# The last product of the scan moves from GpSimd to VectorE, and an output projection moves behind the last sums on TensorE

## The reference, cut to what matters

```
def step(h, inps):
    dt_t, x_t, B_t, C_t = inps
    dA = jnp.exp(dt_t[..., None] * A)
    h = h * dA + (dt_t * x_t)[..., None] * B_t[:, None, :]
    y = jnp.einsum('bdn,bn->bd', h, C_t)
    return (h, y)
_, ys = jax.lax.scan(step, h0, xs)
y = jnp.moveaxis(ys, 0, 1)
y = y + xc * D_param
y = y * jax.nn.silu(z)
mamba_out = y @ out_proj_w.T
residual = mamba_out + residual
hs = rmsnorm(residual, ln_ff_w)
...                                   # router, top 2 of 8 experts, experts
```

## Time and profile before

| | |
|---|---|
| median of three executions | 639.96 us (639.33 to 641.60) |
| profiled execution, device time | 641.04 us |
| its span, first to last instruction | 639.3 us |
| mean granted TensorE clock | 0.991 |
| PE busy | 592.2 us, 93% |
| DVE busy | 460.7 us, 72% |
| ACT busy | 387.9 us, 61% |
| POOL busy | 293.8 us, 46% |
| scan (first to last product on POOL) | 80.1 to 231.8 us |

### The profile page before, as it was taken

How to read it: one execution, slowest core, us unless ns; L and a number is a source line. 1 busy time by engine, 2 the same in 40 slices (tenths; PEclk the granted TensorE clock), 3 DMA queues, 4 the chain that set the end, 5 groups by cost and what they waited for, 6 DMA issues and landing times.

```text
span 639.3 us, 11082 instructions
## 1 busy us (share of the span) xinstructions
PE 592.2 (93%) x3725; PEld 466.4 (73%) x3725; DVE 460.7 (72%) x770; ACT 387.9 (61%) x876; POOL 293.8 (46%) x232
## 2 busy tenths in 40 slices
PE   4999779988999999999999999999999999999774
PEld 2653679988898888798889889899855555655442
DVE  6989989999999956534435442642575698999985
ACT  4589899999999956532223231311546665768543
POOL 6023599999999992222231333152113233133301
PEclk9999799999999999999999999999999999999998
DMA  8001552212121108424413441411520000000001
GB/s 283 2 1 36 159 222 63 55 52 65 50 59 58 34 7 331 138 111 173 162 52 149 158 172 41 165 34 33 172 108 1 2 1 0 1 2 1 1 0 66
DMA packets 18193, 51.44 MB, mean 80 GB/s; under 512 B 3779, under 2 KB 9540, under 8 KB 16485
## 3 DMA queue, kind: packets, MB, share of 16 engines
q1 hardware_dynamic: 15172, 41.43, 18.7%
q0 software_dynamic: 2688, 7.34, 4.0%
q10 hardware_dynamic: 288, 2.10, 0.9%
HBM read 45.95 MB, written 4.92 MB: 80 GB/s over the span
## 4 chain that ended last, share of the span: by engine, by line
PE 67%; ACT 13%; DVE 9%; issue 5%; DMA 3%; POOL 1%; POOLq 0%; DVEq 0%; ACTq 0%
PE ps L2067 13%; PE ps L2140 8%; PE ps L2075 7%; ACT arena L653 7%; PE ps L2129 4%; PE ps L2161 3%; ACT arena L668 3%; DMA moe_out<-arena,result_now 3%; PE ps L1884 3%; PE ps L1869 3%; PE ps L1966 2%; PE ps L1915 2%; PE ps L1710 2%; PE ps L2090 2%; PE ps L1719 2%
## 5 line engine op out<-in xcount | busy, mean ns | idle before, releaser
L442 POOL TENSOR_TENSOR arena<-arena 128x1024 f32<-128x1024 f32 x64 | 149.5, 2381 | 4.1 <-DVE arena L1262 3.8
L1262 DVE TENSOR_TENSOR_SCAN arena<-arena,ps 128x1024 f32<-128x1024 f32 x64 | 143.5, 2278 | 4.7 <-ACT arena L653 1.4
L2067 PEld LDWEIGHTS ps<-arena 128*128 128x128 f32 x924 | 106.1, 192 | 5.2 <-issue 4.1
L2067 PE MATMUL ps<-arena 128*128 128x128 f32 x924 | 107.4, 276 | 0.9 <-DVE arena L1360 0.3
L839 ACT ACTIVATE arena<-ps 128x256 f32<-128x256 f32 x63 | 24.1, 383 | 107.3 <-PE ps L2067 107.3
L653 ACT ACTIVATE arena<-arena,a_neg 128x510 f32<-128x510 f32 x128 | 84.6, 710 | 1.9 <-DVE arena L1262 1.7
L1869 PE MATMUL ps<-ident,arena 128*128 128x128 f32 x384 | 65.0, 279 | 9.9 <-ACT arena L664 9.0
L1884 PE MATMUL ps<-ident,arena 128*128 128x128 f32 x512 | 67.0, 273 | 2.2 <-DVE arena L1271 1.8
L668 ACT ACTIVATE arena<-arena,b_tok 128x512 f32<-128x512 f32 x96 | 64.9, 710 | 0.0
L1884 PEld LDWEIGHTS ps<-ident,arena 128*128 128x128 f32 x512 | 57.9, 141 | 3.3 <-DVE arena L1271 1.3
L2140 PE MATMUL ps<-arena 128*128 128x512 f32 x128 | 58.2, 595 | 0.0
(11 more groups left out here) (296 smaller groups left out, 1069.0 us busy)
## 6 DMA issues: line engine op xcount, KB each, us to landing
arena<-in_w_moe SPq DMA_DIRECT2D x8, 2176.0 KB, 9.3
arena<-c_dram SPq DMA_DIRECT2D x32, 256.0 KB, 3.2
arena<-in_w_o ACTq DMA_DIRECT2D x1, 2048.0 KB, 14.3
arena<-in_w_qT SPq DMA_DIRECT2D x1, 2048.0 KB, 10.3
arena<-moe_out SPq DMA_DIRECT2D x8, 256.0 KB, 5.1
arena<-in_w_q SPq DMA_DIRECT2D x1, 2048.0 KB, 10.5
x<-in_x SPq DMA_DIRECT2D x2, 512.0 KB, 4.4
arena<-in_w_in SPq DMA_DIRECT2D x2, 512.0 KB, 5.7
```

The source lines that it names most:

```text
L442: pool.tensor_tensor(in_chunks(hC[unit % 3]), in_chunks(h[unit % 3]), c_bc[:, m % C_BUFS, :].unsqueeze(1).to_broadcast([P, 2, HALF]), ALU. ...
L1262: nc.vector.tensor_tensor_scan(h[unit % 3], dA[:, k, :], ps[:, 2 * k:2 * k + 2, :].rearrange("p a b -> p (a b)"), 0.0, ALU.mult, ALU.add). ...
L2067: ins = nc.tensor.matmul(ps[:, bank, c * P:(c + 1) * P], w13[:, k, chunk * P:(chunk + 1) * P], xT[:, k, :], start=(k == 0), stop=(k == KD ...
```

## The change

VectorE makes the product of the last unit (63) itself, right behind its last scan and ahead of the second half's gate products. POOL's loop ends one unit earlier. The product has no semaphore of its own: it counts `scan_done` up to 65, and TensorE's last sum waits for that value. The new instruction waits for the scan just ahead of it, for the row of C, and for the sum of unit 60, whose buffer of `hC` it writes over.

On TensorE the two matmuls of tile 0 that stood in pass 63 go behind the last sum, where they join the other two. The wait for the last scan and the turning round of blocks 2 and 3 are then the first things in pass 63.

```
--- before.py
+++ after.py
@@ -433,7 +433,7 @@
-            for unit in range(UNITS):
+            for unit in range(UNITS - 1):
                 m = unit // 2
                 pool.wait_ge(s["scan_done"], unit + 1)
...
@@ -1270,10 +1270,20 @@
+            def last_state_times_c():
+                unit = UNITS - 1
+                m = unit // 2
+                dve.wait_ge(s["scan_done"], UNITS)
+                dve.wait_ge(s[f"ld_c{m % C_BUFS}"], 16 * (m // C_BUFS + 1))
+                dve.wait_ge(s["y_summed"], unit - 2)
+                nc.vector.tensor_tensor(hC[unit % 3].rearrange("p (c t) -> p c t", c=2), h[unit % 3].rearrange("p (c t) -> p c t", c=2),
+                                        c_bc[:, m % C_BUFS, :].unsqueeze(1).to_broadcast([P, 2, HALF]), ALU.mult).then_inc(s["scan_done"], 1)
+
             for unit in range(UNITS):
                 scan_of(unit)
                 if unit == UNITS // 2 + 2:
                     times_gates(0)
+            last_state_times_c()
             times_gates(1)
@@ -1887,7 +1897,10 @@
-                pe.wait_ge(s["hc_done"], unit + 1)
+                if unit < UNITS - 1:
+                    pe.wait_ge(s["hc_done"], unit + 1)
+                else:
+                    pe.wait_ge(s["scan_done"], UNITS + 1)
@@ -1926,9 +1939,6 @@
                 else:
-                    if unit == UNITS - 1:
-                        pe.wait_ge(s["ld_late"], 32)
-                        project_out(0, (0, 1))
                     pe.wait_ge(s["scan_done"], unit + 1)
                     transpose_gated(0, range(2 * (unit % 2), 2 * (unit % 2) + 2))
@@ -1937,7 +1947,8 @@
             sum_states(UNITS - 1)
-            project_out(0, (2, 3))
+            pe.wait_ge(s["ld_late"], 32)
+            project_out(0, range(CI))
             project_out(1, range(CI))
```

## The result

The changed kernel takes 654.37 us (median of 6, 652.88 to 654.91) against 640.85 us of the kernel before (median of 6, 639.33 to 641.91). The ratio is 1.0206, with a 95% interval of 1.0188 to 1.0225: 2.1% slower, where I forecast 0.06% faster and gave "slower" a chance of 0.08. The profiled execution took 653.03 us, its span is 651.2 us.

The account below looks back on a forecast made before the run. TensorE's chain around the last scan's end was taken to bound the kernel; the second half's turning round would move from 237.18 to 236.79. Median 639.96 - 0.39 = 639.57, so 639.6 us, range 638.6 to 641.7.

Parts of the forecast that it names:

- slower: Whole kernel measurably slower, over 641.88 us, about 0.3% above the kernel before; chance 0.08.
- number (3): Last sum, unit 63, waits for VectorE's product, held by POOL's unit 62 product; product ends 230.52, sum starts 230.58.
- rival C: POOL's masks go before VectorE's product: one mask 1.92 us slower, chance 0.07; all four 9.4 us more, chance 0.02.
- rival B: VectorE slips in between POOL's reads, pushing POOL's product of unit 62 by up to 1.22 us; 0.63 us slower, chance 0.10.
- TensorE would fill its gap with the turning round: Behind the sum of unit 61, blocks 2 and 3 turn round 228.05 to 228.92; sum of unit 62 starts 229.50.
- Twenty-four rows at 0.2225 us: TensorE's projections of tiles 0, 1 and 2 behind the last sum take 5.34 us, to 236.79.
- VectorE's product makes the last sum startable 1.23 us earlier: At TensorE's sum of unit 63: replacing POOL's last product by VectorE's lets it start 1.23 us earlier.
- The gain of 0.39: Second half's turning round on TensorE at 236.79 instead of 237.18, with the 0.39 us arriving whole at the kernel's end.
- rivals with a long wait: Last sum waits for VectorE's product behind POOL's masks: 1.92 us slower for one, 9.4 us for all; chances 0.07, 0.02.
- Rival C once: POOL's first mask alone goes before VectorE's product; second turning round at 239.10, 1.92 us slower, 641.9 us; chance 0.07.
- the expensive case: POOL keeps the ports through all four masks; VectorE's product ends 240.30, kernel takes 9.4 us more, 649.4; chance 0.02.

Follow-up runs that it names:

- Experiment 6: Changed kernel, one-tensor TENSOR_SCALAR replacing POOL's first mask (last scan to second turning round 9.10 us), VectorE's last product (that instruction 11.90 us), or both (3.57 us).
- experiment 5: Changed kernel with VectorE's last product reading its second input from PSUM instead of the row of C; that product took 1.22 us.
- experiments 1 and 2: Changed kernel with POOL's first mask waiting for VectorE's product: 0.9994 of the kernel before; the change's parts alone: TensorE's order 1.0028, VectorE's product 1.0175.
- the long wait: Changed kernel with POOL's first mask waiting for VectorE's last product; D (last scan's end to second half's turning round) 9.36 us, ratio to kernel before 0.9994.
- the short one: Changed kernel with POOL waiting only for its own product of unit 62 before its first mask; last scan's end to second turning round took 9.34 us.
- experiment 3: Changed kernel with POOL waiting for VectorE's product behind its first mask, not ahead of it; ratio to the kernel before 1.0048, D 12.98 us.
- experiment 4: Changed kernel with POOL waiting only for its own product of unit 62 before its first mask; D 9.34 us, executed once, no ratio.

## Why the prediction was wrong

The step that failed is number (3) of the change, VectorE's product: "VectorE stands still until 0.14 us before POOL's end and then runs", with POOL's end taken as 229.44, the end of the product of unit 62. The distance to POOL's end was right (1.08 us, in every TENSOR_TENSOR run above to 0.01) and "POOL's end" was wrong. It is the end of everything of two tensors that POOL has queued without a wait, 237.95 in the profile after. I had priced exactly this as rival C, "through all four masks": the turning round at 246.57, which is D = 19.05, and 9.4 us more; I gave it 0.02. Measured: VectorE's product ended 12.69 behind the last scan and the sum started 12.75 behind it, which at the full clock gives D = 12.75 + 6.21 = 18.96.

Two readings of mine led there.

- In the earlier trace rows, POOL had nothing queued behind its product. At 552 its next instruction came 2.36 us later, behind a wait for VectorE. In the changed kernel four instructions were queued. These rows could say what one POOL instruction costs VectorE, and nothing on who goes next (POOL behind the first of them):

```profile
554.59 0.55 POOL L513 TENSOR_TENSOR tile_rs<-tile_var,neg_half 128x1 f32<-128x1 f32 x1 [2.36 <-DVE tile_var L1496]
```

- In the earlier trace rows, I used the one place with a queued successor, and its successor was of another form. L394 is a TENSOR_SCALAR, the masks are TENSOR_TENSOR. Experiment 6 shows that exchanging this form is enough to let VectorE in. I had noted the difference under rival B, and did not carry it over to rival C.

The rule of the Trainium skill (SBUF — State Buffer, Who interferes with whom), that the issue order decides, led the same way, and this case does not bear it out: VectorE's row begins at 226.38, the masks' rows at 228.21 and later, and VectorE went last. The other half, that two SBUF inputs on VectorE conflict with GpSimd's reads, the traces bear out (1.22 us with one input in PSUM, experiment 5; 12.65 us with two in SBUF).

Point by point of the rest:

- That TensorE would fill its gap with the turning round and start the sum of unit 62 with POOL's product: right (226.90 and 228.30 in the profile after, 0.56 and 1.96 behind the last scan; forecast 0.53 and 1.98).
- Twenty-four rows at 0.2225 us: right wherever the clock was up (5.34 us in experiments 1 and 2), 6.91 us after the change.
- "VectorE's product makes the last sum startable 1.23 us earlier": right once POOL waits (product ends 3.03 behind the scan, POOL's ended 4.23 behind it).
- The gain of 0.39: 0.30 in D with the long wait, 0.32 with the short one; in the total time it is too small to be seen.
- The price of rivals with a long wait: too low. I priced the wait and not the clock behind it, 2.46 us for the 9.7 us of idle time, and 1.39 us for the 2.3 us of experiment 3. Rival C once was put at 1.92 us and measured at 3.3 in D.
- The chance of 0.08 for "slower" was too small in another way: the conflict was known, POOL's queue behind it was known, and apart from the rule one place of the trace, with another form of instruction, was all that spoke against the expensive case.

## What to carry to other kernels

Before work moves to VectorE beside a busy GpSimd, list what GpSimd has queued behind its current instruction without a wait: a VectorE product of two SBUF tensors waited here for all of it, and not for one. If it must be there, make GpSimd wait once, be it for its own last instruction, which left a gap of 0.08 us on GpSimd, made its next instruction 0.9 us longer and brought the product from 12.65 us to 2.97; or give VectorE one of its inputs in PSUM (1.22 us). None of these made this kernel measurably faster than before; they took the loss away. And a wait that leaves TensorE idle is priced with the lower clock behind it, which here added 2.46 us to a 9.7 us wait.

## What the runs showed of the hardware that I had not expected

- Instructions of GpSimd that each read two tensors and follow one another without a stop held VectorE off for 11 us, five in a row (the profile after); a gap of 0.08 us between two of them let it in (experiment 4).
- With a TENSOR_SCALAR of one tensor next on GpSimd, a VectorE product of two SBUF inputs went ahead without any wait of GpSimd: it ended 1.1 us behind GpSimd's product, and the TENSOR_SCALAR took 3.82 us (experiment 6).
- A TENSOR_SCALAR of VectorE with one tensor from SBUF was shut out nearly as long as the product with two (11.90 us, experiment 6), while a product with an SBUF and a PSUM input was not (1.22 us, experiment 5).
- 2.3 us of idle TensorE, behind a stretch in which it was busy but for 0.36 us, were followed by a stretch with the clock granted at 0.66 (experiment 3); before the change it idled 0.83 us in the same place and kept 1.00.
